# Mode products of a Fourier layer in half-batches inside the pipeline of the layers

## What is computed

```python
h = layer_norm(x @ fc0_w + fc0_b, ln0_g, ln0_b)
h = jnp.transpose(h, (0, 3, 1, 2))
for i in range(LAYERS):                      # 4 layers, WIDTH 32, M1 = M2 = 12
    x1 = spectral_conv(h, w1, w2)            # complex weights of layer i
    x2 = jnp.einsum('bchw,oc->bohw', h, conv_w[i]) + conv_b[i][None, :, None, None]
    h = layer_norm(transpose(x1 + x2), ln_g[i], ln_b[i])
    if i < LAYERS - 1:
        h = gelu(h)
    h = jnp.transpose(h, (0, 3, 1, 2))
...
def spectral_conv(x, w1, w2):
    x_ft = jnp.fft.rfft2(x)
    out_ft = out_ft.at[:, :, :M1, :M2].set(jnp.einsum('bixy,ioxy->boxy', x_ft[:, :, :M1, :M2], w1))
    out_ft = out_ft.at[:, :, -M1:, :M2].set(jnp.einsum('bixy,ioxy->boxy', x_ft[:, :, -M1:, :M2], w2))
    return jnp.fft.irfft2(out_ft, s=(h, w))
```

## Time and profile before

| | us |
|---|---|
| median of three timed runs | 3752.55 |
| lowest and highest | 3745.9, 3754.82 |
| the profiled execution's own time | 3738.8 |
| its span, first to last instruction | 3737.0 |
| stem | 0 to 359 |
| layers one to three with their products | 360 to 2144 |
| last product and last pass | 2144 to 3040 |
| attention and experts | 3040 to 3737 |

### The profile page before, as it was taken

The page is one execution under the profiler, slowest core; times in us unless marked ns, Lnnn a source line. Parts: engine busy times, 40 slices in busy tenths (PEclk is TensorE's granted clock), DMA queues, the critical chain, the costliest instruction groups (busy, mean ns, idle before and its releaser), DMA issues. The chain is left out here.

```text
span 3737.0 us, 200810 instructions
## 1 busy us (share of the span) xinstructions
PE 3328.7 (89%) x86496; PEld 2355.1 (63%) x86496; DVE 2463.3 (66%) x3868; ACT 2241.8 (60%) x3789; POOL 2146.4 (57%) x1148
## 2 busy tenths in 40 slices
PE   7998699999689999769999969999999968888887
PEld 5776477777567777657777744444444426666665
DVE  8897478888368888557888634444444437666665
ACT  5776267777257777347777526777777744454544
POOL 2443378888168888357888614444444425555553
PEclk9999689999789999879999879999999979999988
DMA  3443344444334444334444331111111110000000
GB/s 109 140 142 120 94 134 153 154 153 153 105 111 154 154 153 154 116 104 151 154 154 154 120 88 49 46 53 47 52 46 52 47 36 10 10 11 11 10 11 9
DMA packets 170977, 347.87 MB, mean 93 GB/s; under 512 B 53282, under 2 KB 94818, under 8 KB 170546
## 3 DMA queue, kind: packets, MB, share of 16 engines
q1 hardware_dynamic: 167058, 341.39, 29.3%
q0 software_dynamic: 3744, 3.84, 0.8%
HBM read 187.44 MB, written 157.71 MB: 92 GB/s over the span
## 5 line engine op out<-in xcount | busy, mean ns | idle before, releaser
L1247 POOL TENSOR_TENSOR rstd<-var,mhalf 128x16 f32<-128x16 f32 x512 | 1542.9, 3030 | 941.0 <-DVE var L1025 941.0
L1039 DVE TENSOR_TENSOR zt<-ps,rstd 128x512 f32<-128x512 f32 x512 | 352.4, 688 | 363.4 <-POOL rstd L1247 359.7
L557 PE MATMUL ps<-d,hp 128*32 128x48 f32 x32768 | 479.5, 212 | 45.7 <-issue 20.4
L493 PEld LDWEIGHTS ps<-dyi,gt 64*48 64x48 f32 x16384 | 392.5, 174 | 199.8 <-issue 182.0
L493 PE MATMUL ps<-dyi,gt 64*48 64x32 f32 x16384 | 435.6, 250 | 78.6 <-ACT gt L806 44.7
L557 PEld LDWEIGHTS ps<-d,hp 128*32 128x32 f32 x32768 | 405.7, 113 | 132.3 <-issue 69.6
L784 ACT COPY asb<-ps 128x384 f32<-128x384 f32 x512 | 259.6, 507 | 299.8 <-PE ps L557 299.1
L1025 DVE TENSOR_REDUCE var<-sq 128x16 f32<-128x528 f32 x384 | 403.0, 1050 | 31.8 <-ACT sq L744 31.7
L532 PE MATMUL ps<-ident,hp 128*128 128x128 f32 x2048 | 376.7, 309 | 11.5 <-ACT ho L768 10.2
L482 PEld LDWEIGHTS ps<-cwl,hc 64*64 64x64 f32 x16384 | 276.4, 141 | 147.1 <-issue 137.2
L465 PE MATMUL ps<-zb,ex 48*128 48x512 f32 x1024 | 309.3, 676 | 48.4 <-DVE zb L1085 47.8
(11 more groups left out here) (168 smaller groups left out, 5019.5 us busy)
## 6 DMA issues: line engine op xcount, KB each, us to landing
h_scratch<-ho SPq DMA_DIRECT2D x256, 512.0 KB
hc<-h_scratch SPq DMA_DIRECT2D x256, 512.0 KB, 4.0
wsb<-in_w SPq DMA_DIRECT2D x64, 288.0 KB, 2.9
g_scratch<-gs SPq DMA_DIRECT2D x192, 96.0 KB, 2.3
gt<-g_scratch SPq DMA_DIRECT2D x256, 72.0 KB
tokens<-wsb SPq DMA_DIRECT2D x256, 4.0 KB
xin<-in_x SPq DMA_DIRECT2D x64, 48.0 KB
xs<-tokens SPq DMA_DIRECT2D x64, 35.2 KB
```

The source lines that it names most:

```text
L493: last = nc.tensor.matmul(z[c][64 * u:64 * u + 2 * TRIG, 32 * col:32 * col + 32], gt[b][rows, :, :, :, k].rearrange("k m x s -> k (m x s)" ...
L557: last = nc.tensor.matmul(a_ps[row:row + 32, 2 * TRIG * k:2 * TRIG * k + 2 * TRIG], hp[b][:, u, 8 * j + k].rearrange("p v r -> p (v r)"), ...
L1039: nc.vector.tensor_tensor(by_px(zt[h][:, u]), by_px(main_ps(s, h, u)), scale, ALU.mult).then_inc(norm_ready, 1)
L1247: nc.gpsimd.tensor_tensor(rstd[u][:], var[u][:], mhalf[:], ALU.pow).then_inc(rstd_ready, 1)
```

## The change

`mix` is split by images into two halves of 32 images (`half` 0 and 1), each run at a place inside the stream of steps: half 0 of layer s+1's product before step 24 of layer s, half 1 of layer s's product before step 8 of layer s (its modes are those of the layer before). Half 0 of the first product goes before the last pairs of the stem; half 1 of the last pass's product into its first step. A half has 12 rows (`e`), each of 24 multiplies on 32 rows of output at four tile positions; `gs` has 128 partitions and ROWBUFS = 6; four DMAs store a row. The layers one to three are one stream, `layer_stream`: the step after 31 is step 0 of the next layer, whose neighbours `near` finds across the border. The weights are loaded and centred one chunk a step, in steps 8 to 23. The text's normalisation is cut in two: sums behind the stem, squares before the last pass. `hst`, the output's buffer of the last pass, moves from `wsb` to `hp`.

```diff
-ROWBUFS = 4
+ROWBUFS = 6
...
-        gs = [sb(f"gs{n}", [2 * IMGS, 2, KX // 2, 2, CH]) for n in range(ROWBUFS)]
+        gs = [sb(f"gs{n}", [128, 2, KX // 2, 2, CH]) for n in range(ROWBUFS)]
...
-        hst = [wsb[:, 16 * p:16 * p + 16].rearrange("p m s c -> p (m s c)") for p in range(2)]
+        hst = [hp[p][:].rearrange("p u c v r -> p (u c v r)")[:, 0:1024] for p in range(2)]
...
+        def stored(eng, s, half, e):
+
+            uses = 2 * mix_number(s, half) + e // ROWBUFS
+            at_least(eng, g_out[e % ROWBUFS], 64 * uses)
...
+        def mix_banks(s, half):
+
+            if isinstance(s, int) and half == 0 and s == 1:
+                return 5, 4, 7
+            if isinstance(s, int) and half == 1 and s == LAYERS:
+                return 2, 3, 4, 5
+            return 4, 5, 6, 7
...
+            couple(step, COUPLES - 1, 2)
+            mix()
+            couple(step, COUPLES, 2, drain)
...
+        def layer_stream(eng, step, mix):
+
+            def body(s):
+                with eng.Fori(2, 8) as g:
+                    step(s, g)
+                mix(s, 1)
+                with eng.Fori(8, 14) as g:
+                    step(s, g, g - 8)
+                step(s, 14, 6)
+                with eng.Fori(15, 24) as g:
+                    step(s, g, g - 8)
+                mix(s + 1, 0)
+                with eng.Fori(24, 30) as g:
+                    step(s, g)
+                step(s, 30)
+                step(s, 31)
+            step(1, 0)
+            step(1, 1)
+            with eng.Fori(1, LAYERS - 1) as s:
+                body(s)
+                step(s + 1, 0)
+                step(s + 1, 1)
+            body(LAYERS - 1)
+            step(LAYERS - 1, 32)
+            step(LAYERS - 1, 33)
...
+            def mix(s, half):
+
+                for e in range(KY // 2):
+                    sp.wait_ge(gs_ready, KY // 2 * mix_number(s, half) + e + 1)
+                    waits_apart(sp, passed)
+                    for b in range(2):
+                        for r in range(2):
+                            row = 64 * b + 32 * r
+                            sp.dma_start(g_dram[32 * half:32 * half + 32, 2 * e + r, :, b, :],
+                                         gs[e % ROWBUFS][row:row + 32].rearrange("i g x s c -> i g (x s c)")
+                                         ).then_inc(g_out[e % ROWBUFS], 16)
...
+            def layer_mix(s, half):
+
+                n = rank(s, 8) if half else rank(s - 1, 24)
+                pe.wait_ge(hc_ready, 4 * n - 6)
+                pe.wait_ge(a_ready, 4 * n - 4)
+                for c in range(2):
+                    pe.wait_ge(zb_ready[c], n - PAIRS + 1)
+                pe.wait_ge(x_ready, n - 2)
+                mix(s, half)
+
+            def mix(s, half):
+
+                banks, before = mix_banks(s, half), KY // 2 * mix_number(s, half)
+                pe.wait_ge(x_ready, PAIRS * (s - 1) + PAIRS // 2 * (half + 1))
                 pe.wait_ge(w_cent, COUPLES * s)
+                pe.wait_ge(dc_ready, half + 1)
+                images = slice(IMGS // 2 * half, IMGS // 2 * half + IMGS // 2)
+                for e in range(KY // 2):
+                    if e >= len(banks):
+                        pe.wait_ge(gs_ready, before + e - len(banks) + 1)
+                    waits_apart(pe, passed)
+                    for a in range(6):
+                        for r in range(2):
+                            for b in range(2):
+                                k, row, mode = slice(64 * b, 64 * b + 64), 64 * b + 32 * r, KY * a + 2 * e + r
+                                last = nc.tensor.matmul(
+                                    ps[row:row + 32, banks[e % len(banks)], 64 * a:64 * a + 64],
+                                    xsb[k, mode, images], wsb[k, mode].rearrange("k s c -> k (s c)"),
+                                    start=True, stop=True, tile_position=(64 * b, row))
+                    last.then_inc(mix_ready, 1)
+
+                pe.wait_ge(gs_ready, before + KY // 2)
...
-            with pe.Fori(1, LAYERS) as s:
-                mix(s)
-                i1(s, 0, 0, 16)
-                layer(s)
...
+            i1(1, 0, 0, 16)
+            layer_stream(pe, layer_step, layer_mix)
```

More of the change, by code:

```diff
@@ L372, in step, with last_pass @@
+            def last_pass(s):
                 def step(i, p, h):
                     g = 2 * i + p
[L374 to L396, removed]
+                    if isinstance(i, int) and i == 0 and p == 0 and h == 1:
+                        mix(s, 1)
+                        stored_all(sp, s, 1)
@@ L591, in step @@
                         turn(STEM, t[1], 2 * t[0] + t[1], h, 1)
[L592 to L629, removed]
@@ new lines, in stem, with layer_step, of @@
+                with_mix(pe, step, 3, first_mix)
+            def layer_step(s, g, chunk=None):
+                here, nxt = (near(s, g, 0), near(s, g, 1)) if not isinstance(g, int) or g < PAIRS else (None, None)
+                old, older = near(s, g, -1), near(s, g, -2)
+                def of(pair, op, *rest):
+                    if pair:
+                        op(pair[0], 0, pair[1], *rest)
+                of(here, widen, 0)
+                of(older, turn, 1, 0)
+                of(here, conv, 0)
+                of(older, turn, 1, 1)
+                of(older, f2, 0)
+                of(old, turn, 0, 0)
+                of(older, f2, 1)
+                of(old, turn, 0, 1)
+                of(here, widen, 1)
+                of(here, conv, 1)
+                for j, piece in enumerate(((0, 6), (6, 11), (11, 16), None)):
+                    of(old, f1, j)
+                    if nxt and piece:
+                        i1(*nxt, *piece)
@@ L816, in step @@
                     if old:
[L817 removed]
+                        a_copy(STEM, 2 * old[0] + old[1], 2 * old[2], old[1])
                     if t:
@@ L906, in _ @@
             act.wait_ge(late_in, NLATE)
-            with act.Fori(1, LAYERS) as s:
-                conv_weights(s)
-                for c in range(2):
-                    gt_part1(s, 0, c)
-                z_copy(s, 0)
-                layer(s)
+            conv_weights(1)
+            for c in range(2):
+                gt_part1(1, 0, c)
+            z_copy(1, 0)
+            layer_stream(act, layer_step, lambda s, half: None)
             conv_weights(LAYERS)
```

330 lines of the change are left out of this document (167 added, 163 removed).

## The result

The changed kernel takes 3797.02 us (median of four runs, 3786.73 to 3808.4) beside 3753.69 us for the kernel before: ratio 1.0136, 95% interval 1.0109 to 1.0163, so 43 us slower. A second comparison of the same two kernels gave 1.0141 (1.0105 to 1.0177). The profiled execution took 3801.17 us, 62.4 more than the profiled one of before.

The account below looks back on a forecast made before the run. TensorE was taken to bound even steps, with waits for code on first runs. 108 + 14.5 + 17.7 + 15 + 193.0 - 290.7 = +57.5 us, giving 3810 us with the profile-to-median difference of 13.8; range 3700 to 3870.

Parts of the forecast that it names:

- Code that is new (193.0): TensorE's first runs of step code: 57.2 us in layer one, 67.9 each in layers two and three; 193.0 slower.
- the instruction packets: Sign in the profile after: packets in nearly every stretch of a layer, several times the 147 of before.
- The half products (108): Six half products inside the stream of steps, 18 us each, none beside other TensorE work: 108 us slower.
- The bounds, 15.5 and 21: Time of one half product: 15.5 us at 0.38 us per store DMA issued by SP, 21 at 0.61.
- rival B: Products give code time to arrive: steps 8 and 24 even, a half product 15.5 us; total 3737 us; chance 0.22.
- POOL's last chunk (17.7): Before step 24, TensorE's half product waits 5.9 us for POOL to centre the last weights, three times: 17.7 us slower.
- the chunks' steps (15): Steps 8 to 23, one weight chunk each: POOL takes 0.31 us over an even step, 15 us slower in three layers.
- the half in the last pass (14.5): Half product in the last pass's first step, partly covered by a TensorE wait for POOL and VectorE: 14.5 us slower.
- What goes (290.7): Borders between layers, before the last pass and at the stem vanish or shrink: 290.7 us saved.
- the 64.6: Border from layer three to the last pass: 64.6 us saved of 94.2, since draining steps and first batches stay.
- The stem: Border from stem to layer one: step 0 begins at 386 us instead of 425, 39.6 us saved.
- rival A: Slow first steps are an idle pipeline filling and its clock, not code; only layer one's 20.5 stays: 3638 us; chance 0.14.

Follow-up runs that it names:

- the probe: Kernel with loops across the border, later half product and nine row buffers, but TensorE's six half products loop three turns of four rows: 3637.49 us, ratio 0.9700.

## Why the prediction was right

**The step that decided it held:** each first run of a step's code on TensorE is slow. The forecast had 193 us for it, and without them the change would have been faster. The forecast of +57.5 us against the profiled execution stands beside +62.4 measured. The difference of medians is smaller, 43 and 53 in the two comparisons, so 3797 and not 3810: the term that was wrong there is the 13.8 us between profile and median of before, added to a kernel whose profiled execution was 4 us above its own median. That the sum came within 5 us is partly luck. Its parts missed by up to 14 us, the half products and the stem to the slow side, the new code and the last pass to the fast side, and the misses largely cancel.

**Code that is new (193.0).** Over even steps (15.55, or 16.0 with a chunk) the steps at new code cost 54.9 us in layer one, 68.5 in layer two and some 61 in layer three (step 31 there is lost in the drain and taken at 5): 184. The predicted parts were 57.2 and 67.9 for each of the others. That it is code, and not a filling pipeline, is shown by the cut loop and by the loops across the border. By the prediction's terms layers one and two came to 601.7 and 612.4 us; they took 603.6 and 617.9; layer three came to 642.0 and took 634.6. One sign failed: the instruction packets were said to become several times the 147, and they are 220, one and a half times.

**The half products (108).** Measured 60.4 us before step 8 and 61.7 before step 24, so 122 in six, 20.3 each instead of 18. The bounds, 15.5 and 21, held, but the working gave the half to the multiplies and the stores alone. Its own code, which stood only under rival B, is worth more: the probe took 4.5 us off a half, the nine buffers 3. An issue of a 64-piece store took 0.427 us, against 0.38 taken; that is the view by tile:

```profile
L397 SPq DMA_DIRECT2D g_scratch<-gs x384: 315/427/2079, 348.0 to 2288.5; - x192
```

**POOL's last chunk (17.7)** is 19.4 in the list of waits; **the chunks' steps (15)**, up to 16.0 us each against 15.55, came to about 15; **the half in the last pass (14.5)** made the first half of pair 0 there 28.0 us long instead of 13.6: 14.4. (The working's 3.5 should have been 3.8, which is 5.2 less two copies of 0.7.) From there to the end of the kernel 5 us came back.

**What goes (290.7).** The borders went as said. The last one is 45.2 us from step 31's widening to the last pass's, 48 less than before; the other 16.6 of the 64.6 are layer three's first steps in their old form. The stem gave back 29.7 of 39.6. The part that failed is the drain behind the first half product: 15 us, as before, was taken for it. Rows of the timeline there:

```profile
366.35 1.51 PE L616 MATMUL ps<-d,hp 128*32 128x48 f32 x64 [3.35 <-DVE gs L1269]
...
382.53 2.76 PE L630 MATMUL ps<-cy,asb 128*64 128x24 f32 x48 [0.69 <-ACT xsb L861]
...
389.74 0.51 ACT L870 COPY gt<-gt 24x384 f32<-24x384 f32 x1 [3.72 <-DMA gt<-g_scratch]
```
```profile
348.00 29.74 SPq L397 DMA_DIRECT2D g_scratch<-gs  x48
...
382.94 12.52 SPq L385 DMA_DIRECT2D gt<-g_scratch  x4
```

The product ends at 366, not 363; its drain takes 19 us, to 385.3; and gt's loads stand behind the 29.7 us of stores, the stores of h and the loads of hc, so that the copy of gt waits for them until 389.74. The sum had put the stores beside TensorE and not asked when SP would come to gt.

**The rule that spoke the other way.** The idle "issue" of 45.0 us on the products, and a step of 23.7 us that takes 15.8 in a loop, contradict the Trainium skill, page "Runtime: NRT & Kernel Launch", section "Instruction fetch mechanics", where the cost of crossing a boundary between code blocks is "mostly hidden". Here each of these new steps pays 3 to 8 us, the low clock included. Had that cost been hidden, the sum would have given rival A's 3638 us. The page's preference for full unrolling is not borne out either: of the forms of the changed kernel, those with fewer steps written out on TensorE were the faster ones.

## What to carry to other kernels

Where small multiplies follow one another without a pause, as here, new code can cost more than the bubble that a new order removes. Count the places at which TensorE meets a new step, take their price from a first turn in the trace, and set it against that bubble. Joining stages across a border paid here only where the joined steps stayed in one loop: 1.4% slower with five steps written out in each layer, 1.2% faster with none at the borders. The engines need not share one shape of loops.

## What had not been expected of the hardware

A loop of steps with 584 multiplies each ran at full pace from its third turn on (about 15.5 us a step, 16.0 with a chunk), but the first turn behind a product of 576 multiplies took 17.8 to 27.5 us in every run of the changed order. One cut in a loop, with the same work, order and waits, cost 29 instruction packets of about 16 KB and 32 us in three layers. ACT and VectorE, with code written out at the same border, hardly held TensorE up (0.8 us in one step). The instruction queue tells less than it seems to: TensorE stood for "issue" nearly 100 us in one stem without a packet more. And 11.6 us less of issuing on the queue that every load stands in brought no time that the medians show: the waits for loads went, and where the halves were short, waits for ACT, which now issued the other half of the stores, took their place.
